# Part of a piecewise-linear curve moved from TensorE and ScalarE to GpSimd, and absolute values from VectorE to ScalarE, in a graph layer's feed-forward

## What is computed

```python
def pwlin_gelu_basic(x, mantissa_bits_in, mantissa_bits_out):
    xq = float2fix(x, mantissa_bits_in)              # round to multiples of 1/256
    y = jnp.interp(xq, _PWL_X, _PWL_Y)               # 33 breakpoints on [-4, 4]
    y = jnp.where(xq > 4.0, xq, jnp.where(xq < -4.0, jnp.float32(0.0), y))
    return float2fix(y, mantissa_bits_out)
...
h = jnp.einsum('bsd,df->bsf', x, w1) + b1            # 1024 -> 512
h = float2fix(h, MANT_BITS)
h = pwlin_gelu_basic(h, MANT_BITS, MANT_BITS)
out = jnp.einsum('bsf,fd->bsd', h, w2) + b2          # 512 -> 1024
return float2fix(out, MANT_BITS)
```

## Time and profile before

| what | value |
| --- | --- |
| three runs | 3114.61, 3122.33, 3126.99 us; median 3122.33 |
| profiled execution | 3121.2 us, of which its span is 3119.3 us |
| granted TensorE clock, mean | 0.991 |
| TensorE busy | 3043.7 us (98%) |
| VectorE busy | 2609.1 us (84%) |
| ScalarE busy | 1165.6 us (37%) |
| GpSimd busy | 804.5 us (26%), none of it in the feed-forward |
| feed-forward | 2716.7 us to 3119.3 us |
| stores of gat, issued by GpSimd | 100, median 2.6 us from issue to landing; the last issued at 2721.1 us |

### The profile page before, as it was taken

The page is one execution under the profiler, slowest core; times in us unless marked ns, Lnnn a source line. Parts: engine busy times, 40 slices in busy tenths (PEclk is TensorE's granted clock), DMA queues, the critical chain, the costliest instruction groups (busy, mean ns, idle before and its releaser), DMA issues. The chain is left out here.

```text
span 3119.3 us, 41250 instructions
## 1 busy us (share of the span) xinstructions
PE 3043.7 (98%) x14012; PEld 2505.8 (80%) x14012; DVE 2609.1 (84%) x4513; ACT 1165.6 (37%) x1499; POOL 804.5 (26%) x716
## 2 busy tenths in 40 slices
PE   7999999998999999899999999999999999999998
PEld 6888888866888888677778888888888788878887
DVE  6777777766777777698989999999999988788886
ACT  3111111121111111233346566556556544565554
POOL 1266666664666666200000000000000000000000
PEclk9999999999999999999999999999999999999999
DMA  9933333353444444555655356447446534223331
GB/s 330 385 91 70 60 60 60 73 122 80 87 81 98 86 89 94 158 170 169 183 168 159 111 153 167 131 129 195 127 117 173 162 93 117 75 88 106 106 103 53
DMA packets 184432, 395.83 MB, mean 127 GB/s; under 512 B 78181, under 2 KB 79061, under 8 KB 184310
## 3 DMA queue, kind: packets, MB, share of 16 engines
q1 hardware_dynamic: 106230, 308.58, 33.6%
q0 software_dynamic: 71440, 65.24, 11.1%
q10 hardware_dynamic: 6640, 20.45, 1.9%
HBM read 303.36 MB, written 90.81 MB: 126 GB/s over the span
## 5 line engine op out<-in xcount | busy, mean ns | idle before, releaser
L1577 PE MATMUL G_acc<-values,whole_plain 125*125 125x257 f32 x5000 | 1098.5, 382 | 15.0 <-DVE whole_plain L1521 8.9
L1577 PEld LDWEIGHTS G_acc<-values,whole_plain 125*125 125x125 f32 x5000 | 937.8, 188 | 165.2 <-DVE whole_plain L1521 11.3
L375 POOL DMA_INDIRECT counts<-E_twins_now,E_cells_now x392 | 674.4, 1720 | 310.8 <-DMA counts<-E_twins_now,E_cells_now 165.8
L1421 ACT ACTIVATE whole_plain<-whole_plain,G_asrc_slope 125x750 f32<-125x750 f32 (+1 forms) x400 | 377.4, 945 | 387.9 <-DVE whole_plain L1508 386.9
L1508 DVE SCALAR_TENSOR_TENSOR whole_plain<-whole_plain,G_asrc_most 125x750 f32<-125x750 f32 (+1 forms) x400 | 411.5, 1029 | 33.3 <-PE G_acc L1577 32.2
L1393 POOL DMA_DIRECT2D gat<-xT_plain x100 | 53.9, 539 | 1028.6 <-ACT xT_plain L1437 1028.6
L268 PE MATMUL Q_q_ps<-whole,xT_space 128*125 128x512 f32 x1200 | 287.3, 398 | 9.2 <-DVE xT_space L296 9.2
L268 PE MATMUL V_v_ps<-whole,xT_space 128*125 128x512 f32 x1200 | 285.0, 399 | 8.0 <-DVE xT_space L296 4.2
L1049 DVE SCALAR_TENSOR_TENSOR N_least<-xT_plain,asrc_all,N_least 125x750 f32<-125x750 bf16 (+1 forms) x292 | 291.4, 998 | 0.0
L268 PE MATMUL K_k_ps<-whole,xT_space 128*125 128x512 f32 x1200 | 287.0, 398 | 3.2 <-PEq L494 3.2
L268 PE MATMUL Q_mix_ps<-Q_mixer,xT_space 128*125 128x512 f32 x1200 | 284.8, 396 | 4.7 <-DVE xT_space L296 4.7
(11 more groups left out here) (193 smaller groups left out, 3189.7 us busy)
## 6 DMA issues: line engine op xcount, KB each, us to landing
whole_plain<-counts SPq DMA_DIRECT2D x279, 328.1 KB
counts<-wo_raw POOLq DMA_DIRECT2D x50, 763.5 KB, 9.8
whole_plain<-counts SPq DMA_DIRECT2D x68, 382.8 KB
xT_whole<-xnT SPq DMA_DIRECT2D x50, 500.0 KB, 4.1
E_row<-edge_keys ACTq DMA_DIRECT2D x26, 512.0 KB
xnT<-xT_whole SPq DMA_DIRECT2D x25, 500.0 KB
V_xT_other<-xnT SPq DMA_DIRECT2D x25, 500.0 KB, 4.0
gat<-xT_plain POOLq DMA_DIRECT2D x100, 125.0 KB, 2.6
```

The source lines that it names most:

```text
L375: nc.gpsimd.indirect_dma_start(out=counts_cells, out_offset=bass.IndirectOffsetOnAxis(ap=self.cells_now[:, slot, c:c + 1], axis=0), in_=se ...
L1421: nc.scalar.activation(here, here, ACT.Exp, bias=asrc_slope[:, u % H, j:j + 1]).then_inc(exp_ready, 1)
L1577: m = nc.tensor.matmul(acc[0:T, t, 0:CW], weight[:, k % RING, t * T:(t + 1) * T], values[:, u % H, j, :], start=(j == 0), stop=(j == NT - 1))
```

## The change

The curve's last four ramps, all with negative kinks, are no longer terms of the matmul sum. ScalarE makes each as max(-kink x |h| + kink x knot, 0), that is already scaled by minus its kink, into a buffer of its own (folded), and GpSimd subtracts the four from hid, one after the other, in place. Before that ScalarE replaces hid by max(hid, 0), so that L1835 becomes a plain addition. The absolute value is made by ScalarE (Abs) and no longer by VectorE; the minimum stays with VectorE, in a step of its own (level), behind rows_low. Eight terms and eight matmuls remain. folded has one buffer, so ScalarE waits for the previous tile's subtractions (folded_in) before it makes new ones, and VectorE waits for them before the addition. folds(pool) is GpSimd's last work, behind its wait for the stores of gat. The folded values of magnitude are still cut at 918/256.

```diff
--- before.py
+++ after.py
@@ -1411,6 +1411,7 @@
                     broadcast(u + 1)
             store(UN - 1)
             pool.wait_ge(gat_stored, 16 * banks_before(UN))
+            fed.folds(pool)
 
         @block.scalar
         def _(act):
...
@@ -1623,9 +1624,12 @@
     w2 = a["whole"][:, 1, :, :, :].rearrange("p s k n -> p (s k n)").rearrange("p (s k n) -> p s k n", s=2, k=FB)
     spent = a["whole"][0:T, 0, :, :, :].rearrange("p s k n -> p (s k n)")
     least = a["nearest"].least[:, 2:4, :].rearrange("p u w -> p (u w)")
-    KN = len(CURVE)
+    KN, FOLDED = len(CURVE) - 4, 4
+    assert all(kink < 0.0 for _, kink in CURVE[KN:])
     terms = spent[:, 0:KN * F].rearrange("p (i f) -> p i f", i=KN)
     kinks = spent[:, KN * F:KN * (F + T)].rearrange("p (i t) -> p i t", i=KN)
+    folded = (a["whole_plain"][0:T, 0, :, :, :].rearrange("p s k n -> p (s k n)")[:, 8192 - FOLDED * F:8192]
+              .rearrange("p (i f) -> p i f", i=FOLDED))
     kinks_whole = least[:, 2 * WIDEST - KN * T:2 * WIDEST].rearrange("p (i t) -> p i t", i=KN)
     x1, xn, stats, moments, root, knots, kink_row = (first[n] for n in ("x1", "xn", "stats", "moments", "root", "knots", "kink_row"))
     base_in, gat_in, raw1, xT, w1 = (first[n] for n in ("base_in", "gat_in", "raw", "xT", "w1"))
@@ -1640,7 +1644,8 @@
 
     in_loaded, xn_ready, turned, xT_high, xT_low = sem("in_loaded"), sem("xn_ready"), sem("turned"), sem("xT_high"), sem("xT_low")
     hid_done, hid_fixed, size_ready = sem("hid_done"), sem("hid_fixed"), sem("size_ready")
-    terms_ready, bent_done = sem("terms_ready"), sem("bent_done")
+    size_made, terms_ready, bent_done = sem("size_made"), sem("terms_ready"), sem("bent_done")
+    folded_ready, folded_in, fold = sem("folded_ready"), sem("folded_in"), sem("fold")
     gelu_ready, gelu_turned, gelu_high, gelu_low = sem("gelu_ready"), sem("gelu_turned"), sem("gelu_high"), sem("gelu_low")
     fed_done, fed_free = sem("fed_done"), sem("fed_free")
     fed_fixed, out_ready, out_stored, out_free = sem("fed_fixed"), sem("out_ready"), sem("out_stored"), sem("out_free")
@@ -1715,8 +1720,23 @@
     def constants(pool):
         nc.gpsimd.memset(root[:, :], 0.0).then_inc(constants_set, 1)
         for i, (knot, kink) in enumerate(CURVE):
-            nc.gpsimd.memset(knots[:, i:i + 1], -knot / 256.0).then_inc(constants_set, 1)
+            scale = 1.0 if i < KN else -kink
+            nc.gpsimd.memset(knots[:, i:i + 1], -knot / 256.0 * scale).then_inc(constants_set, 1)
             nc.gpsimd.memset(kink_row[:, i:i + 1], kink).then_inc(constants_set, 1)
+
+    def folds(pool):
+        chain = Chain(pool, fold)
+
+        def body(g, n):
+            here = hid[:, n % 2, :]
+            for i in range(FOLDED):
+                chain.settle()
+                pool.wait_ge(folded_ready, g * (FOLDED + 1) + (i + 2))
+                taken = nc.gpsimd.tensor_tensor(here, here, folded[:, i, :], ALU.subtract)
+                if i < FOLDED - 1:
+                    chain.step(taken)
+            taken.then_inc(folded_in, 1)
+        over_tiles(pool, body, chain=chain, steps=FOLDED - 1, **TILES)
 
     def rows_high(act, g):
         act.wait_ge(turned, g + 1)
@@ -1729,8 +1749,19 @@
         high(nc, w1[:, blocks_of(part), 0, :], raw1[:, blocks_of(part), :]).then_inc(w_high[0], 1)
 
     def scalar(act):
+        def make_size(g, n):
+            act.wait_ge(hid_fixed, g + 1)
+            nc.scalar.activation(magnitude[:, n % 2, :], hid[:, n % 2, :], ACT.Abs).then_inc(size_made, 1)
+
         def make_terms(g, n):
+            here = hid[:, n % 2, :]
             act.wait_ge(size_ready, g + 1)
+            nc.scalar.activation(here, here, ACT.Relu).then_inc(folded_ready, 1)
+            if fixed(g, 1):
+                act.wait_ge(folded_in, g)
+            for i in range(FOLDED):
+                nc.scalar.activation(folded[:, i, :], magnitude[:, n % 2, :], ACT.Relu, bias=knots[:, KN + i:KN + i + 1],
+                                     scale=-CURVE[KN + i][1]).then_inc(folded_ready, 1)
             if fixed(g, 1):
                 act.wait_ge(bent_done, g)
             for i in range(KN):
@@ -1740,9 +1771,10 @@
             act.wait_ge(w_loaded[1][half], 16)
             high(nc, w2[:, 0, blocks_of(half), :], raw2[:, blocks_of(half), :]).then_inc(w_high[1], 1)
 
-        act.wait_ge(constants_set, 1 + 2 * KN)
+        act.wait_ge(constants_set, 1 + 2 * len(CURVE))
         act.wait_ge(kinks_made, 1)
         high(nc, kinks[:, :, :], kinks_whole).then_inc(kinks_ready, 1)
+        make_size(0, 0)
         second_weights(0)
         rows_high(act, 1)
         make_terms(0, 0)
@@ -1750,6 +1782,8 @@
         def body(g, n):
             if fixed(g, 0, NT - 3):
                 rows_high(act, g + 2)
+            if fixed(g, 0, NT - 2):
+                make_size(g + 1, n + 1)
             if not fixed(g, 1):
                 second_weights(1)
             if fixed(g, 0, NT - 2):
@@ -1770,13 +1804,13 @@
         if fixed(g, 1):
             dve.wait_ge(turned, g)
         else:
-            dve.wait_ge(constants_set, 1 + 2 * KN)
+            dve.wait_ge(constants_set, 1 + 2 * len(CURVE))
         to_normal(nc, chain, x1[:, n % RING, :], xn[:, :], stats, moments, root, stats_seen).then_inc(xn_ready, 1)
 
     def make_kinks(dve):
-        dve.wait_ge(constants_set, 1 + 2 * KN)
+        dve.wait_ge(constants_set, 1 + 2 * len(CURVE))
         nc.vector.tensor_tensor(kinks_whole, ident[0:T, 0:T].unsqueeze(1).to_broadcast([T, KN, T]),
-                                kink_row[:, :].unsqueeze(2).to_broadcast([T, KN, T]), ALU.mult).then_inc(kinks_made, 1)
+                                kink_row[:, 0:KN].unsqueeze(2).to_broadcast([T, KN, T]), ALU.mult).then_inc(kinks_made, 1)
 
     def rows_low(dve, g):
         dve.wait_ge(xT_high, g + 1)
@@ -1806,20 +1840,21 @@
             nc.vector.tensor_tensor(fed[:, :], fed[:, :], x1[:, n % RING, :], ALU.add).then_inc(out_ready, 1)
 
         def hidden(g, n):
-            here, size = hid[:, n % 2, :], magnitude[:, n % 2, :]
+            here = hid[:, n % 2, :]
             dve.wait_ge(hid_done, g + 1)
             chain.step(nc.vector.tensor_tensor(here, hid_ps[:, :], b1_row[:, :], ALU.add))
             chain.settle()
             fix(here, here).then_inc(hid_fixed, 1)
-            dve.wait_ge(hid_fixed, g + 1)
-            chain.step(nc.vector.scalar_tensor_tensor(out=size, in0=here, scalar=-1.0, in1=here,
-                                                      op0=ALU.mult, op1=ALU.max))
-            chain.settle()
+
+        def level(g, n):
+            size = magnitude[:, n % 2, :]
+            dve.wait_ge(size_made, g + 1)
             nc.vector.tensor_scalar(size, size, WHOLE_FROM / 256.0, None, ALU.min).then_inc(size_ready, 1)
 
         rows_statistics(dve, chain, 2, 2)
         dve.wait_ge(biases_loaded, 32)
         hidden(0, 0)
+        level(0, 0)
         rows_low(dve, 1)
         rows_normal(dve, chain, 2, 2)
         second_weights(0)
@@ -1830,10 +1865,12 @@
                 hidden(g + 1, n + 1)
             if fixed(g, 0, NT - 3):
                 rows_low(dve, g + 2)
+            if fixed(g, 0, NT - 2):
+                level(g + 1, n + 1)
             chain.settle()
+            dve.wait_ge(folded_in, g + 1)
             dve.wait_ge(bent_done, g + 1)
-            chain.step(nc.vector.scalar_tensor_tensor(out=gelu[:, :], in0=hid[:, n % 2, :], scalar=0.0, in1=bent_ps[:, :],
-                                                      op0=ALU.max, op1=ALU.add))
+            chain.step(nc.vector.tensor_tensor(gelu[:, :], hid[:, n % 2, :], bent_ps[:, :], ALU.add))
             chain.settle()
             fix(gelu[:, :], gelu[:, :]).then_inc(gelu_ready, 1)
             if not fixed(g, 1):
@@ -1845,7 +1882,7 @@
                 finish(g - 1, n - 1)
             dve.wait_ge(gelu_high, g + 1)
             low(nc, geluT[:, 1, :, :], gelu_tr[:, :, 0:T], geluT[:, 0, :, :]).then_inc(gelu_low, 1)
-        over_tiles(dve, body, chain=chain, steps=1 + LN_STEPS + 1 + 2, **TILES)
+        over_tiles(dve, body, chain=chain, steps=1 + LN_STEPS + 1 + 1, **TILES)
         dve.wait_ge(out_free, NT)
         for half in range(2):
             cols = slice(half * 512, (half + 1) * 512)
...
```

More of the change, by code:

```diff
@@ L1608, in feed_forward_places @@
         b1_row=sb("b1_row", [T, F]), b2_row=sb("b2_row", [T, D]), geluT=sb("geluT", [128, 2, FB, T], F32R), fed=sb("fed", [T, D]))
-Feed = namedtuple("Feed", ("link", "load_first", "load_next", "load_second_weights", "sync", "constants", "rows_high",
+Feed = namedtuple("Feed", ("link", "load_first", "load_next", "load_second_weights", "sync", "constants", "folds", "rows_high",
                            "first_weights_high", "scalar", "rows_statistics", "rows_normal", "make_kinks", "rows_low",
@@ L1910, in tensor @@
         feed(NT - 1)
-    return Feed(link, load_first, load_next, load_second_weights, sync, constants, rows_high, first_weights_high, scalar,
```

(1 more changed line is left out.)

## The result

The changed kernel takes 3129.6 us (median of 22 runs, 3123.8 to 3138.0), the kernel before 3125.5 us (22 runs, 3114.6 to 3131.0). The ratio is 1.0021, with a 95% interval from 1.0012 to 1.0029: a little slower, by 6.5 us by the ratio and 4.1 between the two medians, where 3140 against 3121, 0.6%, was forecast. It lies in the stated range, near rival (b) and not near the likeliest case. The direction was right, the size three to five times too large.

What follows compares the result with a forecast made beforehand. TensorE was taken as the bound, with VectorE close behind and becoming the bound through the change. Start +6.0, 21 tiles +18.2, body 22 -3.1 and body 23 -0.9 made +20.2 on 3121.2, rounded to 3140 us; range 3101 to 3160.

Steps and rivals of the forecast that it cites:

- rival (b): Feed-forward tiles: path held, with a subtraction of 0.94 us or a hold for part of its length; 3122 us, chance 0.21.
- likeliest case: Feed-forward tiles: subtractions of 1.2 us hold VectorE for their whole length and make it the bound; 3140 us, chance 0.47.
- TensorE's tile: Feed-forward tile on TensorE: four of twelve matmuls go, 0.93 us off, leaving 14.32 us.
- VectorE's own tile: VectorE's own work per tile: L1815 goes, 0.72 us off 14.40, leaving 13.68 us.
- ScalarE and the new waits: ScalarE's two more activations per tile, +1.24 us, and the new waits for Abs and folded_in: hidden behind other work.
- a subtraction: One GpSimd subtraction of 512 elements: taken as 1.2 us, between 0.94 and 1.58.
- stall of VectorE per tile: VectorE's Newton steps L198 and L201, held by GpSimd's subtractions: 2.5 us a tile, nearly all from two subtractions.
- VectorE's tile: VectorE's tile with stall: 13.68 + 2.5 = 16.18 us, making VectorE the bound, 0.93 us worse than before.
- start, to the third L1811 / L1845: Start of the feed-forward: tile 0's Abs delays first product 1, later steps follow; third L1811 +6.0 us.
- 21 tiles: The 21 tiles from the third L1811 at 16.18 us each, against 321.6 us before: +18.2 us.
- body 22: Body 22 of the feed-forward: nothing is normalised and nothing stalls; 12.1 us for 15.25, so -3.1.
- the rest: End of the feed-forward: body 23 gives -0.9 us; in the last body the four matmuls are hidden behind finish.

Runs made afterwards that it cites:

- e1: The changed kernel with GpSimd's four subtractions left out, everything else kept; one run of 3104.3 us.
- e3: The changed kernel with the layer norm's Newton steps written with one tensor operand and a per-partition scalar; 0.9961 of the kernel before.
- e8: The changed kernel with ScalarE's eight terms ahead of Relu and the four folds; one run of 3119.5 us.
- e5: The changed kernel with one-tensor-operand Newton steps, tile 0 in the old order, and the last subtraction after the rows are normalised; 3101.2 us, 0.9938 of the kernel before.
- e4: The changed kernel with tile 0's Abs behind second_weights(0) and rows_high(1), and its minimum behind rows_low(1), the old order; 1.0013 of the kernel before.
- e7: The kernel before with only the Newton steps rewritten with one tensor operand; 0.9998 of the kernel before.
- e2: The changed kernel with each GpSimd subtraction replaced by two MEMSETs, which write and don't read; one run of 3104.7 us.
- e6: The changed kernel with three ramps folded and nine made by TensorE; 0.9964 of the kernel before.

## Why the prediction was wrong in size

The steps, in the prediction's order, in us of the feed-forward's 402.6:

| step | forecast | measured |
| --- | --- | --- |
| TensorE's tile | 14.32 | 14.33 (e1) |
| VectorE's own tile | 13.68 | 13.34 (15.41 - 2.07) |
| ScalarE and the new waits | covered | covered in the steady tiles |
| a subtraction | 1.2 | 1.29 |
| stall of VectorE per tile | 2.49 | 2.07 |
| VectorE's tile | 16.18 | 15.41 |
| start, to the third L1811 / L1845 | +6.0 | +4.4 (35.06 for 30.62) |
| 21 tiles | +18.2 | +4.7 |
| body 22 | -3.1 | -3.2 (12.05) |
| the rest | -0.9 | -1.9 |

**The mechanism was right.** Which engine becomes the bound, that two of the eight Newton steps are held for nearly a subtraction each, that two of the four subtractions do it, and what is late then (geluT's low part) are in the trace as foretold. e1 to e3 show the cause: without the subtractions, or with MEMSETs in their place, the tile is 14.3 us again, and without VectorE's second operand the Newton steps are no longer held. Only one of the two held steps was another, the third L198 and not the first L201. The likeliest case is the one that happened, at another size. The measured time's nearness to rival (b) is a coincidence: (b) rested on a subtraction of 0.94 us or a path held for a part of it, and the subtraction takes 1.29.

**The step that failed is "21 x 16.18"**, in two of its terms: the tiles are 13.5 us of the 16 by which the sum missed.

The first is the stall, forecast 0.17 + 1.16 + 1.16 and measured 0.07 + 1.00 + 1.00. I had taken the subtraction too short and yet the hold too long. The held L198 wants to start 0.09 us after the subtraction, and ends 0.02 after the subtraction's recorded end with its own 0.22 us done, so the path is free some 0.2 us before that end: 1.29 - 0.09 - 0.20 = 1.00. L1840 in e8 is like it: it starts 1.12 us before the recorded end of the subtraction and is held for 2.20 - 1.23 = 0.97. Times 20 steady tiles this is 8.4 of the 13.5 us.

The second is VectorE's own tile: 15.41 - 2.07 = 13.34, for 13.68; e5's tiles without a wait give 13.38. (Of the twenty steady tiles the last five are 15.2 us apart, with the two held L198 at 1.15 us, which gives 13.35; why the holds are shorter there was not tried.) Removing L1815 saves more than its 0.72 us. From L1811's start to L1835's was 3.72 - 0.28 of wait = 3.44 us; from L1845's to L1873's it is 2.50, so 0.94 goes. L1811, L1792, L1815 and L1818 each waited for the one before; now rows_low stands between the rounding and the minimum, and instructions that don't depend on each other overlap by some 0.08 us instead of leaving a gap. The turn from geluT's low part to the next tile is 0.09 shorter as well. Times 20 this is 6.8 us, and the two terms make 15.2.

The body-1 tile went the other way: 17.98 us for 16.64 before and 16.18 forecast. I had it as a steady tile. Its holds are other ones, L1826 (1.49 for 0.43) and L1798 (2.33 for 1.22) in place of two L198, but at 2.2 us no larger than a steady tile's. What it has besides are waits: 1.49 us for the rows' high part and 0.73 us for bent_ps. The turning of the rows began only after 4.20 us in which TensorE stood idle, and it and the curve's matmuls ran at a granted clock of 0.60 of full speed (2755.75 to 2762.00), 1.93 us where a steady tile has 1.07; hence both waits. Without subtractions (e1) they are 1.05 and 0.45 us. The tile is 1.8 us over the forecast and brings the two terms' 15.2 to the 13.5 of the table, but for rounding.

**The start** was too high by 1.6 us. First product 1 stood idle 5.05 us, for 5.2, and took 7.61 us, not 8.6; but tile 0's subtractions hold VectorE, so that the second L1845 is late all the same, by 3.4 us for 3.7. Most of the rest, 0.95 us, is the second term again: in body 0 L1873 starts 2.50 us after L1845, where I had 3.45. Of the +4.4, 1.5 go with the order of tile 0 (e4), and 2.3 with the subtractions (in e1 the third start comes 32.75 us after first product 0); the two overlap and are no sum.

**The rest** came 1.0 us lower than forecast, and most of that is luck. Body 23 gave 0.7 us. The other 1.2 are the last product, which stood idle 3.46 us in both kernels and took 7.36 us for 8.55, at another granted clock (busy time by stretch of the kernel before, then of the changed one; the third number from the right is the clock as a share of full speed):

```profile
3106.13:3114.68 8.55, 8.54 (x24) 6.38 (x24) 1.81 (x3) 0.00 (x0) 0.00 (x0) 0.65 0.22 68
...
3115.80:3123.16 7.36, 7.35 (x24) 5.50 (x24) 1.81 (x3) 0.00 (x0) 0.00 (x0) 0.78 0.22 70
```

After the same pause it has 0.65 and 8.6 us again in e5 and e7, and 0.77 and 7.4 us in e1, e4 and e8. So some 1.2 us of what this pair of executions differs by is the clock's and not the change's.

**The rule on the shared path.** The Trainium skill (SBUF — State Buffer, Who interferes with whom) gave the conditions that the runs bear out: two SBUF inputs are held beside a GpSimd instruction that reads and not beside one that only writes (L198: 1.22 us, and 222 ns in e2); with one operand in PSUM, so one in SBUF, it is free (L1836); the fast forms are held by either (L204 in e8, and 1244 ns in e2). Its "for the whole instruction" is 1.00 of a recorded 1.29 us here. The estimate from the Trainium skill (GPSIMD Engine Reference, Elementwise — side-by-side cycle accounting), 1.1 us, was low: the measured subtraction takes 1.29.

## What to carry to other kernels

Work moved to GpSimd that reads SBUF was free here only where VectorE's instructions beside it had one tensor operand, or a second one in PSUM, and weren't of a fast form. The price is paid by whichever VectorE instruction asks next, so a step of one element can cost a full microsecond, and a chain of tiny dependent steps is as bad a neighbour as two large instructions (2.07 us a tile, and 1.93 in e8), since each gap lets GpSimd in again. Look at the order of both engines before the load of either: with the same work, writing the chain with per-partition scalars turned +0.2% into -0.4% here, and placing the last subtraction under a PSUM read, together with tile 0's old order, brought it to -0.6% (the intervals of e3 and e5 overlap).

## What the runs showed of the hardware

- Per-partition scalar operands didn't meet GpSimd's reads: the Newton steps as tensor_scalar took 272 to 276 ns beside subtractions, at a price of 0.05 us each over the two-operand form (219 and 159 ns, now 273 and 214).
- What 24 matmuls take behind a pause went by the granted clock and not by the length of the pause. After 2.76 us idle first product 1 took 7.40 us in the earlier trace rows and 7.39 in e4, both at a mean clock of 0.77, but 5.86 in e5 and 5.92 in e7 at 1.00, that is at 2.4 GHz throughout. After 5.05 us idle it took from 7.41 us at 0.77 (e3) over 7.61 at 0.75 (the changed kernel) to 8.21 at 0.68 (e6): a part of it at 1.2 GHz each time. Why the same pause was followed by either clock no run here shows. Busy time by stretch of first product 1, of the kernel before and of e5:

```profile
2726.22:2733.62 7.40, 7.40 (x26) 5.80 (x27) 5.12 (x15) 6.34 (x11) 0.00 (x0) 0.77 0.37 106
...
2724.06:2729.92 5.86, 5.86 (x26) 4.64 (x27) 5.46 (x14) 5.86 (x10) 4.22 (x3) 1.00 0.05 7
```

- A GpSimd subtraction that finds the path taken is recorded longer itself (1.99 us behind L1798, 2.07 behind L1840), so its mean of 1461 ns in the groups by line is no price; 1.29 us is what it takes in a steady tile, and 1.45 us lie between the starts of two that follow each other (2919.59 and 2921.04).
